# Linear attention with a routed feed-forward tree: keys turned by DMA, not by TensorE

## The chip, the cores and the metric

The kernel runs on one core of a Trainium2 chip. The metric is device time in microseconds of one execution. Matmuls run on TensorE (PE; PEld is its weight load), which writes PSUM; VectorE (DVE) and ScalarE (ACT) read PSUM and SBUF; GpSimd (POOL) works in SBUF alone; SyncE (SP) issues the DMAs.

## The reference, cut to what matters

`x` is 4 x 2048 x 256, fp32, with 16 heads of 64.

```python
xn = layernorm(x)
Q = phi(xn @ Wq + bq); K = phi(xn @ Wk + bk); V = xn @ Wv + bv      # phi = elu + 1
# causal linear attention, token by token, for each head:
KV += outer(k_i, v_i);  Ks += k_i
out_i = (q_i @ KV) / (q_i . Ks + 1e-6)
attn = out @ Wo + bo
# feed-forward: soft routing down a binary tree of depth 8
gate = sigmoid((xn @ Wq_tree.T) @ routers.T)
leaf_prob = products of gate or 1 - gate from the root to each of 256 leaves
ffn = (leaf_prob @ leaf_values) @ Wout.T + Wout_b
result = x + attn + ffn
```

## The kernel before, in words

**Tiling.** The 8192 tokens are 16 blocks (g) of 512. A block has 8 units (p), one for each pair of heads, so there are 128 units n = 8 g + p. Within a unit the 512 tokens are 8 chunks of 64. Projections are done as three products of split fp32 numbers (high x high, high x low, low x high) for each of two tiles of 128 inputs, six matmuls of 512 columns (`split_product`, L652 to L656).

**A unit on TensorE.** It begins with `tiled(n)` (L806), many 64 x 64 matmuls that use quarters of the array: the outputs from the running state (L765), the outer products of keys and values of unit n + 1 (L740, they read `k_tok`, keys with tokens on partitions), the scores of unit n + 1 (L729, they read `kT` and `qT`, features on partitions) and the outputs from the chunk itself (L779). Then comes the whole-array stretch: a hand-written list of fills, `unit_fills(g, p)` (L27), each the content of one of six PSUM banks: W0, W1 (w_pair), S0, S1 (s_pair), O0, O1 (o_pair). In order: a head fill on W1 (at p = 0 the product V1; at p = 1, 2 the transposes xT of the next block's input; at p = 3, 4 the transposes of the leaf probabilities; at p = 5, 6 a gate product), K of unit n + 2 on W0, Q of unit n + 2 on S0, a tail product of values on S1 (p = 0 to 6), kT of unit n + 2 on W0 (four transposes of the keys, L702) and oT on W1 (four transposes of this unit's output, L709). At p = 7 there is neither head nor tail; there oT comes ahead of the first of two long output products y (L667), and kT between the two.

**The other engines** work through the same list in their own queues, in order. ScalarE makes Relu (L407) and Exp (L410) for K and Q, the high half of what is to be split (L400, L430), the copy of the turned keys into `k_tok` (L420), and the copy of the scores into `aT` (L434). VectorE runs `carry(n + 1)` (L585, the running sums over eight chunks), `norm(n)` (L558 to L562), at p = 0 `normalise` (L506), then for each fill `phi` (L520), `low` (L512), `values` (L529) or `low_of_output` (L544). GpSimd masks the scores of unit n + 1 (L329, in two halves), adds the residual at p = 1 (L337), and at p = 7 works out the gates and all levels of the tree (L345 to L362). SP loads x and stores y.

**What sets the order.** Semaphores, counted by bank: `filled` when TensorE has finished a bank, `drained` when its last reader has. TensorE waits in `fill` (L673) for its bank to be drained, in `outer_products_when_ready` (L784) for kT and V, in `scores_when_ready` (L792) for Q and for both S banks, and in the second transpose of oT for the mask of the next unit (L705, L706):

```python
        for c in range(CH):
            if c == 1 and g * PAIRS + i + 1 < UNITS:
                until(a_masked, 2 * (g * PAIRS + i) + 4)
```

Of the kernel before, what the change touches and what calls it, by code (L numbers as in the profile page):

```python
# [7 lines left out]
F32 = mybir.dt.float32  # L8
F32R = mybir.dt.float32r

P = 128
# [15 lines left out]
def unit_fills(g, p, blocks):  # L27

    n = g * PAIRS + p
    ahead = divmod(n + 2, PAIRS) if n + 2 < blocks * PAIRS else None  # L30
# [12 lines left out]
    if p in (5, 6) and more:  # L43
        head, tail = [("gate", p - 5, g + 1)], [("V0", p - 3, g + 1)]

    fills = [(name, W1) for name in head]
    if ahead:
        fills += [(("K", ahead[1], ahead[0]), W0), (("Q", ahead[1], ahead[0]), S0)]
    fills += [(name, S1) for name in tail]
    if p == PAIRS - 1:  # L50

        fills += [(("oT", p, g), W1), (("y", 0, g), O1)]
    if ahead:
        fills.append((("kT", ahead[1], ahead[0]), W0))
    fills.append((("y", 1, g), S1) if p == PAIRS - 1 else (("oT", p, g), W1))
    return fills
# [4 lines left out]
         (("gate", 0, 0), S0), (("gate", 1, 0), S1), (("kT", 0, 0), W0), (("K", 1, 0), W0), (("Q", 1, 0), W1),  # L61
         (("kT", 1, 0), W0)]


def attention_and_tree_layer(nc, x, Wq, bq, Wk, bk, Wv, bv, Wo, bo,
# [45 lines left out]
    with ExitStack() as ctx:  # L111
# [36 lines left out]
        qT = sb("qT", [P, 2, TOK])  # L148
        ex = sb("ex", [P, 2, TOK])
        k_tok = sb("k_tok", [P, CH, P])  # L150
        aT = sb("aT", [P, 2, 2, CH, D])
        snaps = sb("snaps", [P, CHUNKS - 1, AUG])
# [30 lines left out]
        tree_cols = [xn[:, 0:2].rearrange("p c n -> p (c n)"), xn[:, 2:4].rearrange("p c n -> p (c n)"),  # L183
                     k_tok[:, :, :].rearrange("p c n -> p (c n)")]
        leafvT, woutT, routersT = [t.rearrange("p (t n) -> p t n", t=2) for t in tree_cols]
# [39 lines left out]
        a_masked = sem("a_masked")  # L225
        kv_filled = sem("kv_filled")
        sum_ready = sem("sum_ready")
        o_begun = sem("o_begun")
# [28 lines left out]
        def _(sp):  # L257
# [25 lines left out]

            for g in range(BLOCKS):
                if g + 2 < BLOCKS:
                    sp.wait_ge(x_consumed, g + 1)
                    sp.dma_start(x_in[:, g % 2], x_rows[g + 2]).then_inc(x_loaded[g % 2], 16)
                for i in range(2):
                    name = ("y", i, g)
                    sp.wait_ge(drained[bank_of[name]], count_of[name])  # L290
                    sp.dma_start(out_rows[g, :, 2 * i:2 * i + 2, :],
                                 y_buf[:, 2 * i:2 * i + 2, :]).then_inc(y_stored, 16)
            sp.wait_ge(y_stored, 32 * BLOCKS)

        @block.gpsimd
        def _(pool):
# [67 lines left out]
            FIRST_LEVELS = {0: range(0, 5), 1: range(5, 7), 2: range(7, depth)}  # L364

            mask(0)
            gates(0)
            pool.wait_ge(leaf_step, 1)  # L370
            for n in range(UNITS):
                g, p = divmod(n, PAIRS)
                if p == 0 and g + 1 < BLOCKS:
                    inverse_deviation(g + 1)
                    pool.wait_ge(rstd_ready, 2 * g + 4)
                if n + 1 < UNITS:
                    mask(n + 1)
                if p == 1:
                    residual(g)
                    pool.wait_ge(x_consumed, g + 1)  # L380
                if n in FIRST_LEVELS:
                    for l in FIRST_LEVELS[n]:
                        level(l, 0)
                    pool.wait_ge(leaf_step, 2 * FIRST_LEVELS[n][-1] + 3)
                if p == PAIRS - 1 and g + 1 < BLOCKS:
                    gates(g + 1)
                    for l in range(depth):
                        level(l, g + 1)
                    pool.wait_ge(leaf_step, (g + 2) * LEVEL_STEPS)

        @block.scalar
        def _(act):
# [25 lines left out]
            def copy_keys(name):  # L418
                act.wait_ge(filled[bank_of[name]], count_of[name])
                act.activation(k_tok[:, :, :].rearrange("p c n -> p (c n)"), psum_of(name), ACT.Copy)\  # L420
                   .then_inc(drained[bank_of[name]], 1)
# [45 lines left out]
            exponential(("Q", 1, 0))  # L467
            copy_keys(("kT", 1, 0))

            for n in range(UNITS):  # L470
                if n + 1 < UNITS:
                    copy_scores(n + 1)
                for name, _ in unit_fills(n // PAIRS, n % PAIRS, BLOCKS):
                    kind, i, g = name
                    if kind in "KQ":
                        exponential(name)
                    elif kind == "oT":
                        high_of_output(name)
                    elif kind == "kT":
                        copy_keys(name)  # L480
                    elif kind == "xT":
                        high(name, xnT[:, g % 2, 0, i])
                    elif kind == "leaf":
                        high(name, leafT[:, 0, i])
                    elif kind == "gate":
                        half_gates(name)

        @block.vector
        def _(dve):
# [25 lines left out]
            def phi(name):  # L515
                kind, p, _ = name
                slot, dst = (0, kT) if kind == "K" else (1, qT)
                col = p + (PAIRS if kind == "K" else 0)
                dve.wait_ge(exp_ready, exp_count[name])
                dve.scalar_tensor_tensor(out=dst[:, p % 2], in0=psum_of(name), scalar=bias_one[:, col:col + 1],  # L520
                                         in1=ex[:, slot], op0=ALU.add, op1=ALU.max)\
                   .then_inc(drained[bank_of[name]], 1)

            def values(name):
# [89 lines left out]
            carry(0)  # L614
            phi(("Q", 1, 0))

            for n in range(UNITS):
# [4 lines left out]
                if p == 0 and g + 1 < BLOCKS:  # L622
                    normalise(g + 1)
                fills = [name for name, _ in unit_fills(g, p, BLOCKS)]
                for name in values_first(fills, p):
                    kind, i, b = name
                    if kind in "KQ":
                        phi(name)
# [14 lines left out]
        def _(pe):  # L643
# [7 lines left out]

            def split_product(dst, lhs, rhs, tiles):  # L652
                steps = [s for t in range(tiles) for s in passes(lambda a, t=t: lhs(a, t), lambda a, t=t: rhs(a, t))]
                for i, (l, r) in enumerate(steps):
                    last = pe.matmul(dst, l, r, start=i == 0, stop=i == len(steps) - 1)  # L655
                return last  # L656
# [15 lines left out]

            def fill(name):  # L673
                kind, i, g = name
# [3 lines left out]
                if kind in "KQ":  # L678
                    wt = wk if kind == "K" else wq
                    last = split_product(dst, lambda a, t: wt[:, a, t, i * P:(i + 1) * P],  # L680
                                         lambda a, t: xnT[:, g % 2, a, t], KT_)
                elif kind in ("V0", "V1"):
                    half, n = int(kind[1]), 2 * HALF * D
                    last = split_product(dst, lambda a, t: xnT[:, g % 2, a, t, i * P:(i + 1) * P],
                                         lambda a, t: wv[:, a, t, half * n:(half + 1) * n], KT_)
                elif kind in ("xT", "leaf"):
# [13 lines left out]
                elif kind == "kT":  # L700
                    for c in range(CH):
                        last = pe.transpose(dst[:, c * P:(c + 1) * P], kT[:, i % 2, c * P:(c + 1) * P], ident[:, :])  # L702
                elif kind == "oT":
                    for c in range(CH):
                        if c == 1 and g * PAIRS + i + 1 < UNITS:  # L705
                            until(a_masked, 2 * (g * PAIRS + i) + 4)  # L706

# [76 lines left out]
            def outer_products_when_ready(n):  # L784
                g, p = divmod(n, PAIRS)
                until_drained(("kT", p, g))
                if p in (0, HALF):
# [87 lines left out]
            until_drained(("K", 1, 0))  # L875
            fill(("kT", 1, 0))
            until(split_lo_pool, len(LO_POOL))
            until(split_lo, len(LO_VECTOR))

            for n in range(UNITS):  # L880
                tiled(n)
                fills = unit_fills(n // PAIRS, n % PAIRS, BLOCKS)

                first_by_vector = fills[0][0][0] in ("V1", "xT", "leaf")
                for name, bank in fills:
# [12 lines left out]
                    if kind == "y" and i == 0:  # L898
                        for t in range(LT):
                            until_drained(("leaf", t, g))  # L900
                    if kind == "kT":
                        until_drained(("K", i, g))
                    fill(name)

# [24 lines left out]
```

## Time and profile before

| | |
|---|---|
| median of 3 runs | 1276.48 us (1273.93 to 1276.64) |
| the profiled execution, its own time | 1273.15 us |
| its span, first to last instruction | 1271.4 us |
| mean granted TensorE clock | 0.997 |
| busy: PE, PEld, DVE, ACT, POOL | 98%, 87%, 64%, 49%, 29% |

Busy shares are of the span. Matmuls are pipelined, so the duration drawn for one is longer than the distance to the next; the cost of a step on TensorE is read from the starts. "Idle before" in a row, in brackets, is how long the engine stood still ahead of the instruction, and for whom.

### The profile page before, as it was taken

What the parts mean: (1) busy time and instruction counts of PE and PEld (TensorE: products, weight loads), DVE (VectorE), ACT (ScalarE), POOL (GpSimd) and SP (SyncE); (2) the same over time, 40 slices, a digit from 0 to 9 for tenths busy, and PEclk for the clock granted to TensorE, in tenths of its full rate; (3) what the DMA queues carried; (4) which work ended last, traced back from release to release, by engine and by line L of the source; (5) the groups of instructions that cost most, each with busy time, mean ns of one, the idle gap of its engine ahead of it and who ended that gap; (6) DMA issues with size and microseconds to landing.
All of it is one profiled execution on the core that took longest, in us unless ns stands there. A gap on an engine that the chain in (4) does not pass through costs nothing.

```text
span 1271.4 us, 48688 instructions
## 1 busy us (share of the span) xinstructions
PE 1244.6 (98%) x22173; PEld 1105.0 (87%) x22173; DVE 810.3 (64%) x2186; ACT 622.4 (49%) x1007; POOL 374.3 (29%) x590
## 2 busy tenths in 40 slices
PE   5899999999999999999999999999999999999997
PEld 5789888898988989889898988989889898898986
DVE  4675766757576574765757666575765758657473
ACT  4563654536446363653636445364553636536361
POOL 3424232132421413223142321324214132231320
PEclk9899999999999999999999999999999999999999
DMA  6000001000000000001000010000000000000000
GB/s 223 19 3 19 19 2 35 3 18 20 10 28 3 19 19 10 28 3 36 2 19 19 3 35 3 19 20 10 28 3 19 19 18 20 2 19 3 19 3 18
DMA packets 21597, 25.91 MB, mean 20 GB/s; under 512 B 1025, under 2 KB 19728, under 8 KB 21392
## 3 DMA queue, kind: packets, MB, share of 16 engines
q1 hardware_dynamic: 21392, 22.82, 5.5%
q8 instruction: 173, 2.83, 0.9%
q14 instruction: 32, 0.26, 0.1%
HBM read 14.43 MB, written 8.39 MB: 18 GB/s over the span
## 4 chain that ended last, share of the span: by engine, by line
PE 97%; DVE 1%; ACT 1%; DMA 1%; SPq 0%; issue 0%; DVEq 0%
PE s_pair L655 25%; PE w_pair L655 20%; PE o_pair L667 9%; PE s_pair L667 9%; PE o_pair L765 6%; PE kv_pair L740 5%; PE o_pair L779 5%; PE s_pair L729 5%; PE w_pair L709 4%; PE w_pair L702 4%; PE w_pair L689 3%; DMA ffn_tok<-in_L_ffn_Wout_w_dram 1%; DVE snaps L585 0%; SPq L267 0%; PE o_pair L655 0%; ACT ex L407 0%
## 5 line engine op out<-in xcount | busy, mean ns | idle before, releaser
L329 POOL TENSOR_SCALAR_AFFINE_SELECT aT<-aT 64x512 f32<-64x512 f32 x256 | 167.6, 655 | 833.0 <-ACT aT L434 824.7
L655 PE MATMUL w_pair<-xnT,wk 128*128 128x512 f32 x768 | 205.7, 403 | 0.7 <-ACT k_tok L420 0.7
L655 PE MATMUL s_pair<-xnT,wq 128*128 128x512 f32 x756 | 194.0, 392 | 0.0
L434 ACT ACTIVATE aT<-s_pair 128x512 f32<-128x512 f32 x128 | 76.4, 597 | 238.3 <-PE s_pair L729 238.3
L585 DVE TENSOR_TENSOR snaps<-kv_pair,snaps 128x65 f32<-128x65 f32 x768 | 173.3, 226 | 26.4
L520 DVE SCALAR_TENSOR_TENSOR kT<-w_pair,bias_one,ex 128x512 f32<-128x512 f32 x128 | 96.2, 751 | 122.7 <-ACT ex L410 122.6
L655 PEld LDWEIGHTS s_pair<-xnT,wq 128*128 128x128 f32 x756 | 142.1, 188 | 31.4
L655 PE MATMUL s_pair<-wv,xnT 128*128 128x512 f32 x648 | 168.7, 395 | 0.0
L410 ACT ACTIVATE ex<-ex 128x512 f32<-128x512 f32 x256 | 161.8, 632 | 8.1
L407 ACT ACTIVATE ex<-w_pair,neg_bias 128x512 f32<-128x512 f32 x130 | 89.5, 689 | 148.5 <-PE w_pair L655 148.5
L655 PEld LDWEIGHTS w_pair<-xnT,wk 128*128 128x128 f32 x768 | 136.1, 188 | 26.6 <-ACT k_tok L420 1.0
L655 PEld LDWEIGHTS s_pair<-wv,xnT 128*128 128x128 f32 x648 | 121.6, 188 | 28.6
L420 ACT ACTIVATE k_tok<-w_pair 128x512 f32<-128x512 f32 x128 | 76.4, 597 | 143.0 <-PE w_pair L702 143.0
L520 DVE SCALAR_TENSOR_TENSOR qT<-s_pair,bias_one,ex 128x512 f32<-128x512 f32 x126 | 94.3, 748 | 59.6 <-ACT ex L410 59.6
L765 PE MATMUL o_pair<-snaps,qT 64*64 64x65 f32 x3584 | 112.2, 225 | 3.5 <-DVE state L585 3.5
L544 DVE TENSOR_TENSOR oT<-w_pair,oT 128x512 fp32r<-128x512 f32 x128 | 88.3, 690 | 27.4 <-ACT oT L430 27.4
L667 PE MATMUL o_pair<-wo,oT 128*128 128x256 f32 x768 | 94.7, 279 | 0.0
L667 PE MATMUL s_pair<-wo,oT 128*128 128x256 f32 x768 | 94.7, 279 | 0.0
L667 PEld LDWEIGHTS o_pair<-wo,oT 128*128 128x128 f32 x768 | 91.9, 188 | 0.0
L667 PEld LDWEIGHTS s_pair<-wo,oT 128*128 128x128 f32 x768 | 91.9, 188 | 0.0
L562 DVE TENSOR_TENSOR o_tok<-o_pair,rden 128x512 f32<-128x512 f32 x128 | 88.5, 691 | 4.4
L765 PEld LDWEIGHTS o_pair<-snaps,qT 64*64 64x64 f32 x3584 | 83.6, 135 | 8.7 <-issue 8.4
(105 smaller groups left out, 1953.7 us busy)
## 6 DMA issues: line engine op xcount, KB each, us to landing
x_in<-in_L_attn_x_dram SPq DMA_DIRECT2D x16, 512.0 KB, 3.9
out_dram<-y_buf SPq DMA_DIRECT2D x32, 256.0 KB, 2.1
stage<-in_L_attn_Wv_dram SPq DMA_DIRECT2D x2, 512.0 KB, 8.0
stage<-in_L_attn_Wk_dram SPq DMA_DIRECT2D x2, 512.0 KB, 9.6
stage<-in_L_attn_Wq_dram SPq DMA_DIRECT2D x2, 512.0 KB, 10.8
stage<-in_L_attn_Wo_dram SPq DMA_DIRECT2D x2, 512.0 KB, 9.1
bv_all<-in_L_attn_bv_dram SPq DMA_DIRECT2D x1, 512.0 KB, 8.6
ffn_tok<-in_L_ffn_Wq_dram SPq DMA_DIRECT2D x1, 256.0 KB
```

Source lines behind the costliest of these rows:

```text
L329: pool.affine_select(out=part, in_=part, compare_op=ALU.is_ge, fill=0.0, base=0, pattern=[[0, 2 * CH], [1, D]], channel_multiplier=-1).the ...
L407: act.activation(ex[:, slot], psum_of(name), ACT.Relu, scale=-1.0, bias=neg_bias[:, col:col + 1])\
L410: act.activation(ex[:, slot], ex[:, slot], ACT.Exp, scale=-1.0).then_inc(exp_ready, 1)
L420: act.activation(k_tok[:, :, :].rearrange("p c n -> p (c n)"), psum_of(name), ACT.Copy)\
L434: act.activation(aT[:, n % 2].rearrange("p h c q -> p h (c q)"), s_pair[:, :, 0:CH * D], ACT.Copy).then_inc(s_copied, 1)
L520: dve.scalar_tensor_tensor(out=dst[:, p % 2], in0=psum_of(name), scalar=bias_one[:, col:col + 1], in1=ex[:, slot], op0=ALU.add, op1=ALU.max)\
L544: dve.tensor_tensor(oT[:, 1, p], psum_of(name), oT[:, 0, p].bitcast(F32), ALU.subtract)\
L562: dve.tensor_tensor(o_tok[:, :, :, :].rearrange("p b t (h e) -> p b (t h) e", e=D), v[:, :, :, 0:D], rden[:, :, :].unsqueeze(3).to_broadca ...
L585: dve.tensor_tensor(dst, added, so_far, ALU.add).then_inc(sum_ready, 1)
L655: last = pe.matmul(dst, l, r, start=i == 0, stop=i == len(steps) - 1)
L667: last = pe.matmul(dst[:, (c % 2) * hid:(c % 2 + 1) * hid], oT[:, a, t, cols] if t < PAIRS else leafT[:, a, t - PAIRS, cols], wo[:, b, t] ...
L765: last = pe.matmul(output_at(t, h, a), qT[rows_of(h), p % 2, t * P + a * D:t * P + (a + 1) * D], before, start=turn == 0 and half not in b ...
```

## The change

The keys of units 2 and up no longer go through TensorE to be turned. K is projected one unit earlier (three units ahead of its use, not two) and is the first fill of each whole-array stretch, ahead of the head. When VectorE's `phi` has written `kT`, GpSimd takes the 32-bit numbers apart into two planes of 16-bit halves (`take_apart`), SP issues a DMA that transposes both planes (`turn_keys`), and VectorE interleaves the halves into `k_tok` (`put_together`), ahead of the first fill of an S bank in its list. TensorE waits for the mask ahead of the last matmul of the Q product, and for `put_together` ahead of the last matmul of the S1 product (at p = 7 after the first y). The first two units' keys are still turned by TensorE. SP's order is rewritten: stores of a block at the next block's first unit, the load of x at p = 2.

```diff
@@ unit_fills
-    fills = [(name, W1) for name in head]
-    if ahead:
-        fills += [(("K", ahead[1], ahead[0]), W0), (("Q", ahead[1], ahead[0]), S0)]
+    fills = [(("K", keys[1], keys[0]), W0)] if keys else []
+    fills += [(name, W1) for name in head]
+    if queries:
+        fills.append((("Q", queries[1], queries[0]), S0))
     fills += [(name, S1) for name in tail]
+    fills.append((("oT", p, g), W1))
     if p == PAIRS - 1:
-        fills += [(("oT", p, g), W1), (("y", 0, g), O1)]
-    if ahead:
-        fills.append((("kT", ahead[1], ahead[0]), W0))
-    fills.append((("y", 1, g), S1) if p == PAIRS - 1 else (("oT", p, g), W1))
+        fills += [(("y", 0, g), O1), (("y", 1, g), S1)]
@@ buffers
+        k_planes = sb("k_planes", [P, 2, TOK], U16)
+        k_turned = sb("k_turned", [P, 2 * CH, P], U16)
@@ SP
-            for g in range(BLOCKS):
-                if g + 2 < BLOCKS:
-                    sp.wait_ge(x_consumed, g + 1)
-                    sp.dma_start(x_in[:, g % 2], x_rows[g + 2]).then_inc(x_loaded[g % 2], 16)
+            def turn_keys(m):
+                sp.wait_ge(k_apart, m - 1)
+                if m > 2:
+                    sp.wait_ge(k_whole, m - 2)
+                sp.dma_start_transpose(k_turned[:, :, :], k_planes[:, :, :].rearrange("p s t -> p (s t)"))\
+                  .then_inc(k_turned_in, 16)
...
+            turn_keys(2)
+            for n in range(UNITS):
+                g, p = divmod(n, PAIRS)
+                if p == 0 and g:
+                    store(g - 1)
+                if n + 3 < UNITS:
+                    turn_keys(n + 3)
+                if p == 2 and g + 2 < BLOCKS:
+                    sp.wait_ge(x_consumed, g + 1)
+                    sp.dma_start(x_in[:, g % 2], x_rows[g + 2]).then_inc(x_loaded[g % 2], 16)
+            store(BLOCKS - 1)
@@ GpSimd
+            def take_apart(m):
+                g, p = divmod(m, PAIRS)
+                pool.wait_ge(drained[bank_of["K", p, g]], count_of["K", p, g])
+                if m > 2:
+                    pool.wait_ge(k_turned_in, 16 * (m - 2))
+                pool.tensor_copy(k_planes[:, :, :], kT[:, m % 2].bitcast(U16).rearrange("p (t s) -> p s t", s=2))\
+                    .then_inc(k_apart, 1)
+                pool.wait_ge(k_apart, m - 1)
...
                 if n + 1 < UNITS:
                     mask(n + 1)
+                if n + 3 < UNITS:
+                    take_apart(n + 3)
                 if p == 1:
                     residual(g)
@@ ScalarE
-                    elif kind == "kT":
-                        copy_keys(name)
@@ VectorE
+            def put_together(m):
+                dve.wait_ge(k_turned_in, 16 * (m - 1))
+                dve.wait_ge(kv_filled, m)
+                dve.tensor_copy(k_tok[:, :, :].rearrange("p c f -> p (c f)").bitcast(U16)
+                               .rearrange("p (n s) -> p s n", s=2),
+                               k_turned[:, :, :].rearrange("p (s c) f -> p s (c f)", s=2)).then_inc(k_whole, 1)
...
+                apart = True
                 for name in values_first(fills, p):
                     kind, i, b = name
+                    if apart and bank_of[name] in (S0, S1) and n + 2 < UNITS:
+                        put_together(n + 2)
+                        apart = False
@@ TensorE
-            def split_product(dst, lhs, rhs, tiles):
+            def split_product(dst, lhs, rhs, tiles, at_last=None):
                 for i, (l, r) in enumerate(steps):
+                    if at_last and i == len(steps) - 1:
+                        at_last()
...
-                        if c == 1 and g * PAIRS + i + 1 < UNITS:
-                            until(a_masked, 2 * (g * PAIRS + i) + 4)
...
-                until_drained(("kT", p, g))
+                if n < 2:
+                    until_drained(("kT", p, g))
+                else:
+                    until(k_whole, n - 1)
...
+                def masked():
+                    if n + 1 < UNITS:
+                        until(a_masked, 2 * n + 4)
+                def whole():
+                    if n + 2 < UNITS:
+                        until(k_whole, n + 1)
...
-                    if kind == "kT":
-                        until_drained(("K", i, g))
-                    fill(name)
+                    fill(name, masked if kind == "Q" else whole if bank == S1 and kind != "y" else None)
+                    if kind == "y" and i == 0:
+                        whole()
+                masked()
+                whole()
```

## Rows read from the trace of the kernel before

**Rows 1.** The page's part 1 (busy) and part 4 (the ending chain by line).
```profile
PE 1244.6 (98%) x22173; PEld 1105.0 (87%) x22173; DVE 810.3 (64%) x2186; ACT 622.4 (49%) x1007; POOL 374.3 (29%) x590
...
PE s_pair L655 25%; PE w_pair L655 20%; PE o_pair L667 9%; PE s_pair L667 9%; PE o_pair L765 6%; PE kv_pair L740 5%; PE o_pair L779 5%; PE s_pair L729 5%; PE w_pair L709 4%; PE w_pair L702 4%; PE w_pair L689 3%; DMA ffn_tok<-in_L_ffn_Wout_w_dram 1%; DVE snaps L585 0%; SPq L267 0%; PE o_pair L655 0%; ACT ex L407 0%
```

**Rows 2.** Timeline, one unit (p = 3): start us, us, engine, line, instruction.
```profile
608.33 0.27 PE L765 MATMUL o_pair<-state,qT 64*64 64x65 f32 x1
...
610.45 0.66 PE L689 MATMUL w_pair<-ident,ffn_tok 128*128 128x128 f32 x4
...
610.84 1.37 POOL L329 TENSOR_SCALAR_AFFINE_SELECT aT<-aT 64x512 f32<-64x512 f32 x2 [6.37 <-ACT aT L434]
610.86 1.63 PE L655 MATMUL w_pair<-xnT,wk 128*128 128x512 f32 x6
611.14 0.60 ACT L400 ACTIVATE leafT<-w_pair 128x512 fp32r<-128x512 f32 x1 [0.43 <-PE w_pair L689]
...
612.33 1.53 PE L655 MATMUL s_pair<-xnT,wq 128*128 128x512 f32 x6
612.47 0.68 DVE L512 TENSOR_TENSOR leafT<-w_pair,leafT 128x512 fp32r<-128x512 f32 x1
612.53 0.69 ACT L407 ACTIVATE ex<-w_pair,neg_bias 128x512 f32<-128x512 f32 x1 [0.79 <-PE w_pair L655]
613.25 0.63 ACT L410 ACTIVATE ex<-ex 128x512 f32<-128x512 f32 x1
...
613.70 1.56 PE L655 MATMUL s_pair<-wv,xnT 128*128 128x512 f32 x6
...
613.91 0.75 DVE L520 SCALAR_TENSOR_TENSOR kT<-w_pair,bias_one,ex 128x512 f32<-128x512 f32 x1 [0.77 <-ACT ex L410]
...
614.87 0.59 PEld L702 LDWEIGHTS w_pair<-ident,kT 128*128 128x128 f32 x4
615.10 0.60 PE L702 MATMUL w_pair<-ident,kT 128*128 128x128 f32 x4
615.29 0.75 DVE L520 SCALAR_TENSOR_TENSOR qT<-s_pair,bias_one,ex 128x512 f32<-128x512 f32 x1 [0.62 <-ACT ex L410]
...
615.53 0.60 PE L709 MATMUL w_pair<-ident,o_tok 128*128 128x128 f32 x4
...
615.95 0.68 DVE L529 TENSOR_TENSOR v_aug<-s_pair,bv_all 128x512 f32<-128x512 f32 x1
...
616.06 0.27 PE L765 MATMUL o_pair<-state,qT 64*64 64x65 f32 x1
```

**Rows 3.** Timeline of a p = 0 unit, TensorE and VectorE.
```profile
584.16 0.27 PE L765 MATMUL o_pair<-state,qT 64*64 64x65 f32 x1
...
592.86 0.27 PE L765 MATMUL o_pair<-state,qT 64*64 64x65 f32 x1
...
588.57 1.37 DVE L506 TENSOR_SCALAR xn<-x_in,mean_var,rstd 128x256 f32<-128x256 f32 x4
```

**Rows 4.** Groups by line and shape: count, busy us, mean ns.
```profile
L337 POOL TENSOR_TENSOR y_buf<-x_in,y_bias 128x1024 f32<-128x1024 f32 x16 | 38.7, 2419 | 1.3
...
L345 POOL TENSOR_SCALAR ffn_tok<-ffn_tok 128x1024 f32<-128x1024 f32 x16 | 17.6, 1102 | 1.4
...
L242 DVE TENSOR_TENSOR wk<-stage,wk 128x1024 fp32r<-128x1024 f32 x1 | 1.2, 1215 | 0.0
```

**Rows 5.** Timeline of the start, VectorE beside GpSimd.
```profile
37.63 1.38 POOL L329 TENSOR_SCALAR_AFFINE_SELECT aT<-aT 64x512 f32<-64x512 f32 x2 [7.20 <-ACT aT L434]
...
38.48 1.60 DVE L242 TENSOR_TENSOR wo<-stage,wo 128x1024 fp32r<-128x1024 f32 x1 [0.68 <-ACT wo L396]
...
39.10 1.89 POOL L345 TENSOR_SCALAR ffn_tok<-ffn_tok 128x1024 f32<-128x1024 f32 x1
```

**Rows 6.** The page's part 6: DMA issues, KB each, us to landing.
```profile
out_dram<-y_buf SPq DMA_DIRECT2D x32, 256.0 KB, 2.1
...
stage<-in_L_attn_Wq_dram SPq DMA_DIRECT2D x2, 512.0 KB, 10.8
```

More of the change, by code:

```diff
@@ L9 @@
 F32R = mybir.dt.float32r
+U16 = mybir.dt.uint16
 P = 128
@@ L29, in unit_fills @@
     n = g * PAIRS + p
-    ahead = divmod(n + 2, PAIRS) if n + 2 < blocks * PAIRS else None
+    keys = divmod(n + 3, PAIRS) if n + 3 < blocks * PAIRS else None
+    queries = divmod(n + 2, PAIRS) if n + 2 < blocks * PAIRS else None
     more = g + 1 < blocks
@@ L61 @@
          (("gate", 0, 0), S0), (("gate", 1, 0), S1), (("kT", 0, 0), W0), (("K", 1, 0), W0), (("Q", 1, 0), W1),
-         (("kT", 1, 0), W0)]
+         (("kT", 1, 0), W0), (("K", 2, 0), W0)]
 def attention_and_tree_layer(nc, x, Wq, bq, Wk, bk, Wv, bv, Wo, bo,
@@ L183, in attention_and_tree_layer @@
         tree_cols = [xn[:, 0:2].rearrange("p c n -> p (c n)"), xn[:, 2:4].rearrange("p c n -> p (c n)"),
-                     k_tok[:, :, :].rearrange("p c n -> p (c n)")]
+                     k_tok[:, :, :].rearrange("p c f -> p (c f)")]
         leafvT, woutT, routersT = [t.rearrange("p (t n) -> p t n", t=2) for t in tree_cols]
@@ L226, in attention_and_tree_layer @@
         kv_filled = sem("kv_filled")
+        k_apart = sem("k_apart")
+        k_turned_in = sem("k_turned_in")
+        k_whole = sem("k_whole")
         sum_ready = sem("sum_ready")
@@ L282, in _, with store @@
             load("wo1")
-            for g in range(BLOCKS):
-                if g + 2 < BLOCKS:
-                    sp.wait_ge(x_consumed, g + 1)
-                    sp.dma_start(x_in[:, g % 2], x_rows[g + 2]).then_inc(x_loaded[g % 2], 16)
+            def turn_keys(m):
[4 more added lines that the diff above has]
+                  .then_inc(k_turned_in, 16)
+            def store(g):
                 for i in range(2):
@@ L370, in _ @@
             pool.wait_ge(leaf_step, 1)
+            take_apart(2)
             for n in range(UNITS):
@@ L419, in copy_keys @@
                 act.wait_ge(filled[bank_of[name]], count_of[name])
-                act.activation(k_tok[:, :, :].rearrange("p c n -> p (c n)"), psum_of(name), ACT.Copy)\
+                act.activation(k_tok[:, :, :].rearrange("p c f -> p (c f)"), psum_of(name), ACT.Copy)\
                    .then_inc(drained[bank_of[name]], 1)
@@ L468, in _ @@
             copy_keys(("kT", 1, 0))
+            exponential(("K", 2, 0))
             for n in range(UNITS):
@@ L515, in phi @@
             def phi(name):
-                kind, p, _ = name
-                slot, dst = (0, kT) if kind == "K" else (1, qT)
+                kind, p, b = name
+                slot, dst = (0, kT[:, p % 2]) if kind == "K" else (1, qT[:, p % 2])
                 col = p + (PAIRS if kind == "K" else 0)
                 dve.wait_ge(exp_ready, exp_count[name])
-                dve.scalar_tensor_tensor(out=dst[:, p % 2], in0=psum_of(name), scalar=bias_one[:, col:col + 1],
+                dve.scalar_tensor_tensor(out=dst, in0=psum_of(name), scalar=bias_one[:, col:col + 1],
                                          in1=ex[:, slot], op0=ALU.add, op1=ALU.max)\
                    .then_inc(drained[bank_of[name]], 1)
+            def put_together(m):
[4 more added lines that the diff above has]
+                               k_turned[:, :, :].rearrange("p (s c) f -> p s (c f)", s=2)).then_inc(k_whole, 1)
             def values(name):
@@ L615, in _ @@
             phi(("Q", 1, 0))
+            phi(("K", 2, 0))
             for n in range(UNITS):
@@ L671, in output_rows, with fill @@
                 return last
-            def fill(name):
+            def fill(name, at_last=None):
                 kind, i, g = name
@@ L680, in fill @@
                     last = split_product(dst, lambda a, t: wt[:, a, t, i * P:(i + 1) * P],
-                                         lambda a, t: xnT[:, g % 2, a, t], KT_)
+                                         lambda a, t: xnT[:, g % 2, a, t], KT_, at_last)
                 elif kind in ("V0", "V1"):
@@ L684, in fill @@
                     last = split_product(dst, lambda a, t: xnT[:, g % 2, a, t, i * P:(i + 1) * P],
-                                         lambda a, t: wv[:, a, t, half * n:(half + 1) * n], KT_)
+                                         lambda a, t: wv[:, a, t, half * n:(half + 1) * n], KT_, at_last)
                 elif kind in ("xT", "leaf"):
@@ L701, in fill @@
                     for c in range(CH):
-                        last = pe.transpose(dst[:, c * P:(c + 1) * P], kT[:, i % 2, c * P:(c + 1) * P], ident[:, :])
+                        last = pe.transpose(dst[:, c * P:(c + 1) * P], kT[:, i, c * P:(c + 1) * P], ident[:, :])
                 elif kind == "oT":
                     for c in range(CH):
-                        if c == 1 and g * PAIRS + i + 1 < UNITS:
-                            until(a_masked, 2 * (g * PAIRS + i) + 4)
                         to = dst[:, c * P:(c + 1) * P].rearrange("p (a q) -> p a q", a=2)
@@ L876, in _ @@
             fill(("kT", 1, 0))
+            fill(("K", 2, 0))
             until(split_lo_pool, len(LO_POOL))
@@ L882, in _ @@
                 fills = unit_fills(n // PAIRS, n % PAIRS, BLOCKS)
-                first_by_vector = fills[0][0][0] in ("V1", "xT", "leaf")
+                first_by_vector = any(bank == W1 and name[0] in ("V1", "xT", "leaf") for name, bank in fills)
+                def masked():
[4 more added lines that the diff above has]
+                        until(k_whole, n + 1)
                 for name, bank in fills:
```

## The prediction

> **What bounds the kernel now.** I read the page first. TensorE is busy for 98% of the span, and the chain that ended last is made of TensorE's lines almost alone; the transposes of the keys (L702) hold 4% of it [rows 1]. VectorE is busy for 64%. So work taken from TensorE shortens the kernel one for one, until TensorE has to wait. Whether it will is a question of one unit's order in time, so I went to the timeline of a p = 3 unit [rows 2] and of a p = 0 unit [rows 3]. Count time there from the unit's first L765 matmul at 608.33, called 0. The leaf transposes start at 2.12, K at 2.53, Q at 4.00, V at 5.37, kT at 6.77, oT at 7.20, and the next unit at 7.73. Steps: transposes 0.41, K 1.47, Q 1.37, V 1.40, kT 0.43, oT 0.53. The reader is to see in the same rows the keys' path beside TensorE: K's first matmul to Relu 1.67, Relu to Exp 0.72, Exp to phi 0.66; phi starts 3.05 after K does. VectorE idles 0.77 ahead of it. There is slack in VectorE, but not at every place in its queue.
>
> **What the change removes.** 126 of the 128 kT fills on TensorE, 0.43 each by starts [rows 2]: 54 us in all. ScalarE's 126 copies to k_tok go too; ScalarE is half idle [rows 1], so I count nothing for them. Moving the wait for the mask from oT to Q's last matmul costs nothing: the mask starts at 2.51 and takes 1.37 [rows 2], so it ends at 3.88, while Q's last matmul now comes near 5.1.
>
> **What it adds.** Per unit: a GpSimd copy of 1024 16-bit elements, a transposing DMA of 256 KB, a VectorE copy of 1024 elements (`put_together`), and two waits. Three of these must be placed.
>
> *GpSimd.* 29% busy [rows 1]. The copy is bounded by 1.10 us (one input, 1024 elements) and 2.42 us (two inputs) [rows 4]; I take 1.10, the nearer form. Behind it in GpSimd's queue stand the next mask, wanted some 4 us later, and at p = 1 the residual add and at p = 7 the tree levels, which have units of time. It costs nothing by itself.
>
> *DMA and SP.* A 256 KB store lands after 2.1 us; the slowest large load, 512 KB in the crowded start, took 10.8 [rows 6]. No transposing DMA is in the trace. I take it near the store, since it is the same bytes at a quiet time. It is issued when the copy has ended and k_turned is free, near 7.7 of one unit, and wanted near 6.4 of the next, some 7.6 us later. Up to that it is hidden. SP's store waits for y, which is drained about a microsecond into p = 0, and the load at p = 2 stands behind a turn it doesn't need: both are in time. At p = 7 a unit lasts near 20 us and covers everything.
>
> *VectorE.* `put_together` stands in front of the first fill of an S bank, and TensorE now waits for it (k_whole) ahead of the last matmul of the S1 product. That is a wait within the same unit, for data that only the next unit's outer products need. Work out when it can end, at p = 3. K goes first, so it starts at 2.12 and phi(K) at 2.12 + 3.05 = 5.17. The low half of the leaf, which used to run at 4.14 ahead of phi, now stands behind it: two VectorE operations follow each other 0.66 apart for one of 0.75 (615.29 to 615.95) [rows 2], so it starts at 5.84, which ScalarE's copy (0.60, after Exp ends at 5.14) just allows. `put_together` starts 0.60 later, at 6.44. TensorE comes to V's last matmul at 2.12 + 1.47 + 0.41 + 1.37 + 5/6 of 1.40 = 6.54. So TensorE waits for nearly the whole copy, whatever that takes.
>
> Its price: no VectorE copy from SBUF to SBUF of this size is shown. The nearest row, 1024 elements in SBUF, is 1.22 us [rows 4]. Below it is the 0.68 of 512 elements [rows 2]. I take 1.22: the one single-input operation from SBUF to SBUF, L506, does four times 256 elements in 1.37 [rows 3], so one element a cycle of about 1 ns too. Then the copy ends at 7.66; from phi's end (614.66) to the weight load that waited for it are 0.21, and to the matmul 0.23 more [rows 2], so V's last matmul runs at 8.10, oT at 8.33, the next unit starts at 8.86. Against 7.73 that is 1.13 us longer.
>
> The Trainium skill (VectorE: DVE Perf Modes, the perf-mode tier table) says that an fp32 copy or tensor_scalar within SBUF handles two elements per cycle; the L506 row doesn't agree. An estimate by that table's rate is 0.69 us for this copy. The same skill (SBUF — State Buffer, Who interferes with whom) adds what speaks against the change: a VectorE operation in such a mode takes a port pair it shares with GpSimd as an exclusive lock. By both together the copy would wait for `take_apart` to end near 7.2 and itself end near 7.9, and the time would be about 1357.
>
> The trace shows such holding: a subtraction of 1.22 took 1.60 when it started inside a mask, and a GpSimd operation of 1.10 took 1.89 when it started inside that subtraction [rows 4, 5]. Here `take_apart` starts when phi(K) ends, near 6.05, and runs to 7.15, so a `put_together` that needs what GpSimd holds starts near 7.25 instead of 6.44: 0.81 more. A copy has one input, the held subtraction had two; I leave it out of the sum and keep it for the range.
>
> **By kind of unit**, in 16 blocks:
> - p = 1 to 4, 64 units with a low half on W1 or one like it: +1.13 each, +72.3.
> - p = 0, 16 units: `normalise` runs from 588.57 for 1.37 [rows 3], so phi(K) starts at 5.69, values at 6.35, the copy at 6.95; it ends at 8.17, the next unit starts at 8.17 + 0.21 + 0.23 + 0.23 + 0.53 = 9.37, against 8.70 (584.16 to 592.86): +0.67 each, +10.7.
> - p = 5, 6: the head is a gate product, drained by ScalarE; the copy runs from 5.84 to 7.06, and V's last matmul comes near 7.6. p = 7 has no S1 product to hold. 47 units at -0.43: -20.2.
>
> Sum +62.8. The profiled execution took 1273.15 (span 1271.40); 1273.15 + 62.8 = 1336. The median of the runs shown is 3.3 above that execution, so I say 1339.
>
> **Rivals.**
> *Short copy* (0.68, not held): copy ends at 7.12; p = 1 to 4 +0.59, p = 0 +0.13, the rest -0.43: +37.8 + 2.1 - 20.2 = +19.7, 1296. For it: 16-bit data; against it: L506.
> *Long copy, held and of full length*: +0.81 on 80 units, 65 more, 1404. If GpSimd's copy takes 2.42, a held short copy ends near 9.2, 1462.
> *The other side: the wait is already met.* If `put_together` can end before TensorE comes to V's last matmul, all 126 x 0.43 = 54 come out: 1222. It decides where the copy ends before 6.54 - 0.44 = 6.1 at p = 1 to 4. For it: VectorE has 0.77 idle ahead of phi(K) and 36% overall. Against it: its queue is in order, and even a copy of no length stands behind the low half, which ends at 6.4. Ordering or latencies would have to be half a microsecond better than in the rows.
> *Nothing in sum*: a very short copy, about 0.3: p = 1 to 4 +0.2, p = 0 -0.2, the rest -0.43; within 0.2%.
> *The DMA isn't hidden.* One transposition is under way at a time. If it takes 10.8, a unit needs 10.8 + some 0.8; 3.9 more at p = 1 to 4, 2.9 at p = 0, 5, 6: 24 a block, about 1650. It decides from 7.6 us on.
>
> **How the numbers follow.** The forecast's kind, 1310 to 1380: 0.50; short copy 0.18; held long or slow GpSimd, to 1460, 0.08; all saved 0.11; nothing in sum 0.05; DMA unhidden 0.08. The range is 1275 to 1460: it leaves out the two far cases, 0.19. A difference under 0.2% (2.6 us) can't be told from none by this measurement. Faster 0.11, same 0.05, slower 0.84.
>
> **What would show it.** In the profile after: TensorE below 98% with idle ahead of the S1 product's last matmul, put down to VectorE's `put_together`, in p = 0 to 4 and none in p = 5 to 7; units of 8.9 at p = 1 to 4 and 0.4 shorter ones at p = 5 and 6; L702 with 8 instructions; the new VectorE group with a mean of 1.2 (or 0.7, or more when held); a transposing DMA that lands under 7 us. Wrong if phi(K) doesn't start near 5.2, if the low half runs ahead of it, if the copy is far from 1.2, or if SP's waits name the DMA as the last to come.

## The result and the profile after

The changed kernel takes 1312.17 us (median of 4; 1309.35 to 1313.8), the kernel before 1276.56 beside it: ratio 1.0273, interval 1.0251 to 1.0295. It is slower by 36 us. I had said 1339, slower with a chance of 0.84, range 1275 to 1460. The profiled execution took 1312.1, with a span of 1310.3.

The page of the changed kernel: busy shares, the chain by engine, the two new copies and the new DMA (KB are not given for it; 3.1 is us to landing).

```profile
PE 1213.1 (93%) x21669; PEld 1040.4 (79%) x21669; DVE 923.1 (70%) x2312; ACT 552.0 (42%) x881; POOL 529.3 (40%) x716
...
PE 70%; DVE 19%; ACT 7%; issue 3%; DMA 1%; SPq 0%; POOL 0%; DVEq 0%; POOLq 0%
...
L396 POOL COPY k_planes<-kT 128x1024 uint16<-128x1024 uint16 x126 | 149.7, 1188 | 280.6 <-issue 228.9
...
L564 DVE COPY k_tok<-k_turned 128x1024 uint16<-128x1024 uint16 x126 | 133.8, 1062 | 0.0
...
k_turned<-k_planes SPq DMA_TRANSPOSE x126, 3.1
```

TensorE is busy 31.5 us less than in [rows 1], but its share fell from 98% to 93%, and the chain that ends last now runs through VectorE for 19%. Both new means are mixtures: VectorE's copy takes 1.24 in nearly all units of p = 0 to 4 and 0.75 in the others, GpSimd's 1.04 in the first and 1.43 in the second. The DMA lands well inside its time. The waits of the changed kernel, us in total, times, longest, put a name to the loss (PEld is the weight load of the same matmul, so the two lines are one wait):

```profile
PEld s_pair L707 <- DVE k_tok L564: 103.0, 78, 2.0
...
PE s_pair L707 <- DVE k_tok L564: 68.8, 77, 1.5
```

The idle drawn, 68.8 us, is less than what the waits cost, for the drawn length of a matmul runs past the start of the next: the kernel is near 39 us longer although 54 us were taken out, 93 in all.

Where in a unit it stands is seen in the timeline. This is a unit with the same fills as [rows 2] (p = 4 here, p = 3 there), from its first L816 matmul to the next unit's:

```profile
634.26 0.27 PE L816 MATMUL o_pair<-state,qT 64*64 64x65 f32 x1
...
636.28 1.65 PE L707 MATMUL w_pair<-xnT,wk 128*128 128x512 f32 x6
...
637.77 0.60 PE L742 MATMUL w_pair<-ident,ffn_tok 128*128 128x128 f32 x4
...
639.36 0.75 DVE L556 SCALAR_TENSOR_TENSOR kT<-w_pair,bias_one,ex 128x512 f32<-128x512 f32 x1 [0.94 <-ACT ex L447]
...
639.60 1.32 PE L707 MATMUL s_pair<-wv,xnT 128*128 128x512 f32 x5
...
640.02 0.68 DVE L548 TENSOR_TENSOR leafT<-w_pair,leafT 128x512 fp32r<-128x512 f32 x1
640.23 1.04 POOL L396 COPY k_planes<-kT 128x1024 uint16<-128x1024 uint16 x1 [2.17 <-issue]
...
640.62 1.24 DVE L564 COPY k_tok<-k_turned 128x1024 uint16<-128x1024 uint16 x1
...
641.92 0.51 PE L707 MATMUL s_pair<-wv,xnT 128*128 128x512 f32 x1 [0.99 <-DVE k_tok L564]
...
642.26 0.60 PE L760 MATMUL w_pair<-ident,o_tok 128*128 128x128 f32 x4
...
642.79 0.27 PE L816 MATMUL o_pair<-state,qT 64*64 64x65 f32 x1
```

Read it as the prediction counted, with 634.26 as 0. K starts at 2.02, phi of K at 5.10, the low half of the leaf at 5.76, VectorE's copy at 6.36; it ends at 7.60, and the last matmul of the S1 product, the lone L707 row with 0.99 of idle, starts at 7.66. The unit lasts 8.53 instead of 7.73. Two things were not in the sum: the matmul follows the copy's end by 0.06, and the copy's 1.24 is not its own length. GpSimd's copy runs from 640.23 to 641.27, and VectorE's, drawn from 640.62, ends 0.59 after that. In a p = 5 unit of the same execution VectorE starts first, and the roles change:

```profile
648.57 0.74 DVE L564 COPY k_tok<-k_turned 128x1024 uint16<-128x1024 uint16 x1
648.77 1.43 POOL L396 COPY k_planes<-kT 128x1024 uint16<-128x1024 uint16 x1 [2.18 <-issue]
```

There VectorE's copy takes 0.74, and it is GpSimd's that is drawn out, to 1.43. It ends 0.89 after VectorE's.

Unit lengths here and below run from a unit's first L816 matmul (L765 before) to the next unit's, and are medians over the blocks. For p = 0 to 7 they are 9.03, 8.54, 8.53, 8.72, 8.54, 8.22, 8.33 and 19.55; before they were 8.69, 7.73, 7.74, 7.73, 7.74, 8.77, 8.71 and 19.92. The sum per block is 2.43 us more, times 16 blocks 38.9 us, which is the difference between the two profiled spans (1310.3 and 1271.4).

### The profile page after: what moved, and what is told of

The parts are those of the page before. It is cut to its first block, busy times and chain, and to the rows that moved or that the text cites. A ratio compares the mean times of both kernels' runs of the same rounds, so it can differ in the third digit from the quotient of the medians.

```text
span 1310.3 us, 48282 instructions
## 1 busy us (share of the span) xinstructions
PE 1213.1 (93%) x21669; PEld 1040.4 (79%) x21669; DVE 923.1 (70%) x2312; ACT 552.0 (42%) x881; POOL 529.3 (40%) x716
## 4 chain that ended last, share of the span: by engine, by line
PE 70%; DVE 19%; ACT 7%; issue 3%; DMA 1%; SPq 0%; POOL 0%; DVEq 0%; POOLq 0%
PE w_pair L707 17%; PE s_pair L707 11%; PE o_pair L719 9%; PE s_pair L719 8%; DVE k_tok L564 7%; PE o_pair L816 6%; PE kv_pair L791 5%; PE w_pair L760 4%; PE o_pair L830 4%; PE s_pair L780 4%; ACT ex L444 4%; ACT ex L447 3%; DVE kT L556 3%; DVE snaps L629 2%; DVE leafT L548 2%
## 5 line engine op out<-in xcount | busy, mean ns | idle before, releaser
L396 POOL COPY k_planes<-kT 128x1024 uint16<-128x1024 uint16 x126 | 149.7, 1188 | 280.6 <-issue 228.9
L707 PE MATMUL s_pair<-wv,xnT 128*128 128x512 f32 x648 | 189.2, 407 | 68.8 <-DVE k_tok L564 68.8
L707 PEld LDWEIGHTS s_pair<-wv,xnT 128*128 128x128 f32 x648 | 121.5, 187 | 127.8 <-DVE k_tok L564 103.0
L707 PE MATMUL w_pair<-xnT,wk 128*128 128x512 f32 x768 | 211.9, 411 | 2.2 <-ACT k_tok L457 2.2
L707 PE MATMUL s_pair<-xnT,wq 128*128 128x512 f32 x756 | 200.9, 400 | 0.5 <-POOL aT L353 0.2
L707 PEld LDWEIGHTS w_pair<-xnT,wk 128*128 128x128 f32 x768 | 134.3, 188 | 34.2 <-ACT k_tok L457 2.7
L707 PEld LDWEIGHTS s_pair<-xnT,wq 128*128 128x128 f32 x756 | 135.2, 188 | 26.4 <-POOL aT L353 1.4
L467 ACT ACTIVATE oT<-w_pair 128x512 fp32r<-128x512 f32 x128 | 76.3, 596 | 148.7 <-PE w_pair L760 148.7
L564 DVE COPY k_tok<-k_turned 128x1024 uint16<-128x1024 uint16 x126 | 133.8, 1062 | 0.0
L816 PE MATMUL o_pair<-snaps,qT 64*64 64x65 f32 x3584 | 113.4, 224 | 0.3 <-DVE state L629 0.3
L444 ACT ACTIVATE ex<-s_pair,neg_bias 128x512 f32<-128x512 f32 x126 | 86.8, 689 | 49.4 <-PE s_pair L707 49.0
L573 DVE TENSOR_TENSOR v_aug<-s_pair,bv_all 128x512 f32<-128x512 f32 x108 | 74.5, 690 | 30.1 <-PE s_pair L707 30.1
```

Source lines behind the costliest of these rows:

```text
L396: pool.tensor_copy(k_planes[:, :, :], kT[:, m % 2].bitcast(U16).rearrange("p (t s) -> p s t", s=2))\
L444: act.activation(ex[:, slot], psum_of(name), ACT.Relu, scale=-1.0, bias=neg_bias[:, col:col + 1])\
L564: dve.tensor_copy(k_tok[:, :, :].rearrange("p c f -> p (c f)").bitcast(U16) .rearrange("p (n s) -> p s n", s=2), k_turned[:, :, :].rearran ...
L816: last = pe.matmul(output_at(t, h, a), qT[rows_of(h), p % 2, t * P + a * D:t * P + (a + 1) * D], before, start=turn == 0 and half not in b ...
```

## The experiments

The theory after the result: TensorE is held ahead of the S1 product's last matmul by VectorE's interleaving copy, which is late because of its place in VectorE's queue, and later still because whichever of the two 16-bit copies starts second is held by the first. The rivals: the added work on VectorE and GpSimd is the bound wherever it stands; the transposing DMA is late or disturbs; the order of the fills or the move of the mask's wait does it. The kernel before, timed beside them, took 1277.03 for the first four experiments and 1276.33 for the other four.

### The wait, put where the keys are used

```diff
-                    fill(name, masked if kind == "Q" else whole if bank == S1 and kind != "y" else None)
-                    if kind == "y" and i == 0:
-                        whole()
+                    fill(name, masked if kind == "Q" else None)
                 masked()
-                whole()
```

> The changed kernel, with TensorE's wait for the interleaved keys only where they are used (outer products of the next unit), not ahead of the S1 product's last matmul. My theory (TensorE is held in the same unit by a copy that ends 7.6 us into a p = 1 to 4 unit): the 1.0 us of idle ahead of that matmul goes; the outer products come at 7.6 and hardly wait, but Q and V are then drained only at 8.2 and 8.9, and the scores, wanted at 8.4, wait about 0.6 in its place. So a unit of 7.9 to 8.0 instead of 8.5: about 35 us less, 1270 to 1285. Rival (VectorE's and GpSimd's load is the bound, wherever the wait stands): 1305 to 1315.

1265.9 us, ratio 0.9906 (0.9883 to 0.9929): 46 us less than the changed kernel, 4 below the range that I gave, and about 1% faster than the kernel before. So the wait's place cost that much. What is left is seen in its timeline, where a p = 3 unit starts at 604.02 while VectorE is still at the unit before:

```profile
604.02 0.27 PE L816 MATMUL o_pair<-state,qT 64*64 64x65 f32 x1
...
604.26 0.67 DVE L573 TENSOR_TENSOR v_aug<-s_pair,bv_all 128x512 f32<-128x512 f32 x1
...
604.86 0.74 DVE L556 SCALAR_TENSOR_TENSOR qT<-s_pair,bias_one,ex 128x512 f32<-128x512 f32 x1
...
605.08 0.70 PE L791 MATMUL kv_pair<-v_aug,k_tok 64*64 64x65 f32 x32 [0.60 <-DVE v_aug L573]
...
612.12 0.27 PE L816 MATMUL o_pair<-state,qT 64*64 64x65 f32 x1
```

The outer products (L791) have 0.60 of idle; they wait there for the values that VectorE writes last (604.26, 0.67). The unit lasts 8.10; those of p = 1, 2 and 4 last 7.50, 7.95 and 7.96. The scores, which I expected to wait 0.6, wait 0.2 at most. VectorE's copy is still late (it still takes 1.25) and pushes phi of Q and the values behind it into the next unit. The wait in the unit was a cost of its own, but a late copy costs without it too.

### The copy, put first in VectorE's list

```diff
                 fills = [name for name, _ in unit_fills(g, p, BLOCKS)]
-                apart = True
+                if n + 2 < UNITS:
+                    put_together(n + 2)
                 for name in values_first(fills, p):
                     kind, i, b = name
-                    if apart and bank_of[name] in (S0, S1) and n + 2 < UNITS:
-                        put_together(n + 2)
-                        apart = False
```

> The changed kernel, with put_together ahead of all of VectorE's fills of the unit (right behind norm or normalise), nothing else. My theory (the place of the copy in VectorE's queue is the cause): the copy runs near 4.2 us into the unit, in VectorE's idle time, outside GpSimd's copy, takes 0.75, and TensorE's wait is met long before. Nearly all of 54 us comes out against the kernel before: 1222 to 1235. Rival 1 (VectorE's load or the shared hold is the bound): above 1280. Rival 2 (the transposing DMA is too late for this place, since it lands some 3 us into the unit at best): units bound by the DMA chain, 8 us or more, above 1270.

1229.04 us (1228.92 to 1235.26), ratio 0.9633 (0.9605 to 0.9662): 83 us less than the changed kernel and 48 less than the kernel before. Nothing else was moved: VectorE, GpSimd and the DMAs have the same instructions, and the order of the fills on TensorE is the changed one. That rules out their load, the DMA and that order as what cost the time. The timeline from the copy of a p = 3 unit to the starts of the p = 4 and the p = 5 unit:

```profile
593.50 0.75 DVE L564 COPY k_tok<-k_turned 128x1024 uint16<-128x1024 uint16 x1
...
594.52 0.75 DVE L556 SCALAR_TENSOR_TENSOR kT<-w_pair,bias_one,ex 128x512 f32<-128x512 f32 x1 [0.28 <-ACT ex L447]
...
595.19 0.68 DVE L548 TENSOR_TENSOR leafT<-w_pair,leafT 128x512 fp32r<-128x512 f32 x1
595.40 1.04 POOL L396 COPY k_planes<-kT 128x1024 uint16<-128x1024 uint16 x1 [2.19 <-issue]
...
596.16 0.60 PE L757 MATMUL w_pair<-ident,o_tok 128*128 128x128 f32 x4
...
596.69 0.27 PE L813 MATMUL o_pair<-state,qT 64*64 64x65 f32 x1
...
604.07 0.27 PE L813 MATMUL o_pair<-state,qT 64*64 64x65 f32 x1
```

The copy (593.50, 0.75) now lies in the idle time ahead of phi of K, and GpSimd's (595.40, 1.04) far behind it. oT follows the S1 product with no wait, and the unit from 596.69 to 604.07 lasts 7.38. The prediction's nominal 7.30 differs by 0.08; per block 2.97 us come out, of the 3.4 that the removed transposes would give by 0.43 each.

### GpSimd's copy listed with the next unit

```diff
+                if n and n + 2 < UNITS:
+                    take_apart(n + 2)
                 if n + 1 < UNITS:
                     mask(n + 1)
-                if n + 3 < UNITS:
-                    take_apart(n + 3)
```

> The changed kernel, with GpSimd's take_apart of unit n + 2 at the start of unit n's GpSimd work, ahead of the mask, so that it is far from VectorE's copy. My theory (in p = 0 to 4 VectorE's copy of 0.74 us takes 1.24 because it starts inside GpSimd's copy and is held until that ends): the copies are 0.74 everywhere, 80 units are 0.5 shorter, 1265 to 1280. Rival (1.24 is the copy's own length in these units, or DMA traffic makes it so): copies stay at 1.24, 1305 to 1315. If the DMA, issued 3 us into the unit at worst, lands too late, VectorE waits for it and the time rises.

1306.99 us, ratio 1.0232 (1.0204 to 1.0259): 5 less than the changed kernel, whose interval it overlaps (1.0251 to 1.0295), and in the range of the rival. As a test of the hold it failed, by my mistake: GpSimd has nothing in front of it and reaches the copy as soon as the keys are drained, still in the unit before. An entry moved in a queue that idles is not moved in time. Only at p = 1, behind the residual add, and at p = 7, behind the tree levels, is GpSimd kept back. The timeline shows a p = 1 unit's copies and then, for comparison, those of p = 2:

```profile
611.97 0.73 DVE L564 COPY k_tok<-k_turned 128x1024 uint16<-128x1024 uint16 x1
611.98 1.62 POOL L396 COPY k_planes<-kT 128x1024 uint16<-128x1024 uint16 x1
...
612.76 0.50 PE L707 MATMUL s_pair<-wv,xnT 128*128 128x512 f32 x1 [0.49 <-DVE k_tok L564]
...
619.62 1.04 POOL L396 COPY k_planes<-kT 128x1024 uint16<-128x1024 uint16 x1 [2.18 <-issue]
...
620.01 1.24 DVE L564 COPY k_tok<-k_turned 128x1024 uint16<-128x1024 uint16 x1
...
621.31 0.50 PE L707 MATMUL s_pair<-wv,xnT 128*128 128x512 f32 x1 [1.00 <-DVE k_tok L564]
```

At p = 1 VectorE starts 0.01 ahead of GpSimd and takes 0.73, GpSimd 1.62; the matmul waited 0.49 and the unit lasts 8.01 instead of 8.52. At p = 2, with GpSimd ahead, the copy takes 1.24 and the matmul waits 1.00, as before. In 14 of the 16 units of p = 1 the two copies start within 0.03 of each other, and only one of them is drawn out: in eight it is GpSimd's (1.62 to 1.65) and VectorE's takes 0.73 or 0.74; in six it is VectorE's (1.60), GpSimd's takes 1.04 and the unit lasts 8.9. The first kind ends 0.89 after the other copy, the second 0.59. This speaks for the hold.

### Every turn issued twice

```diff
+                sp.dma_start_transpose(k_turned[:, :, :], k_planes[:, :, :].rearrange("p s t -> p (s t)"))\
+                  .then_inc(k_spare_in, 16)
+                sp.wait_ge(k_spare_in, 16 * (m - 1))
                 sp.dma_start_transpose(k_turned[:, :, :], k_planes[:, :, :].rearrange("p s t -> p (s t)"))\
                   .then_inc(k_turned_in, 16)
```

> The changed kernel, with each transposing DMA issued twice in turn, the second after the first has landed, so the keys come some 3 us later and the DMA work is doubled. My theory (the DMA is hidden; it has 7 us and takes 3.1): no change, 1308 to 1316. Rival (the transposing DMA or its traffic costs the time): each of seven units in eight 1 to 3 us longer, above 1400.

1340.6 us, ratio 1.0488 (1.0456 to 1.052): 28 more than the changed kernel. Both expectations missed; mine was that it is free. Its waits name GpSimd's copy behind the DMA (us, times, longest), and the timeline shows one such place:

```profile
POOL k_planes L400 <- DMA k_turned<-k_planes: 144.0, 45, 5.1
```

```profile
621.11 1.24 SPq L297 DMA_TRANSPOSE k_turned<-k_planes  x1
...
625.70 1.91 SPq L300 DMA_TRANSPOSE k_turned<-k_planes  x1
...
629.17 0.74 DVE L568 COPY k_tok<-k_turned 128x1024 uint16<-128x1024 uint16 x1 [0.77 <-DMA k_turned<-k_planes]
629.29 1.51 POOL L400 COPY k_planes<-kT 128x1024 uint16<-128x1024 uint16 x1 [3.54 <-DMA k_turned<-k_planes]
```

The first turn is issued at 621.11, the second at 625.70, 4.6 later instead of 3.1, and the keys are there near 629.1, 8.0 after the first issue. VectorE waited 0.77 and GpSimd 3.54, and since both are let go by the same landing, they meet again and GpSimd's copy is held (1.51). So the time from issue to use is near 7 to 8 us: one turn of 3.1, or 4.9 at most, fits in it with room, two don't always. That was the flaw in my expectation: twice 3.1 already fills most of it. Why a turn sometimes takes 4.6 I haven't found. For the changed kernel itself the DMA is hidden; its VectorE never waits for it.

### GpSimd's copy only after VectorE's

```diff
                 if m > 2:
                     pool.wait_ge(k_turned_in, 16 * (m - 2))
+                    pool.wait_ge(k_whole, m - 2)
```

> The changed kernel, with one more wait in take_apart: GpSimd copies unit n + 3's keys only after put_together of unit n + 2, so the two copies never overlap. The theory of the hold: VectorE's copy takes 0.74 in every unit, ends 0.5 earlier in 80 units, and the time falls by about 40 to 1272 (1265 to 1280). Rival (the copy is 1.24 long in p = 0 to 4 for another reason): 1305 to 1315. The DMA is issued some 0.6 us later and stays hidden.

1275.45 us (10 runs), ratio 0.9995 (0.9982 to 1.0007): 37 less than the changed kernel, by one added wait, and level with the kernel before. The timeline of a p = 2 unit:

```profile
605.57 0.73 DVE L565 COPY k_tok<-k_turned 128x1024 uint16<-128x1024 uint16 x1
...
606.36 0.50 PE L708 MATMUL s_pair<-wv,xnT 128*128 128x512 f32 x1 [0.49 <-DVE k_tok L565]
606.47 1.04 POOL L397 COPY k_planes<-kT 128x1024 uint16<-128x1024 uint16 x1 [3.08 <-DVE k_tok L565]
```

VectorE's copy takes 0.73, GpSimd's starts behind it and takes 1.04, and the matmul's idle is 0.49 where it was 1.00. Over all 126 the means are 0.75 and 1.04. The hold is shown: it was 0.5 us in each of 80 units, 40 us, close to all that the changed kernel lost. The 0.49 that is left, for a copy that is still late in VectorE's queue, is why this kernel is level with the one before and not at 1229.

### The mask's wait moved, in the kernel before

```diff
-                        if c == 1 and g * PAIRS + i + 1 < UNITS:
-                            until(a_masked, 2 * (g * PAIRS + i) + 4)
...
-                    fill(name)
+                    fill(name, masked if kind == "Q" else None)
+                masked()
```

> The kernel before, with only its wait for the mask moved from oT's second transpose to the last matmul of the Q product. The mask ends 3.9 us into the unit, ahead of both places. Mine: no difference, within 3 us of the kernel before. Rival (a wait among short instructions costs issue time, about 0.1 us a unit): 8 to 15 us faster.

1275.74 us (12 runs), ratio 0.9995 (0.9982 to 1.0008): no difference within 0.2%. That part of the change is neutral.

### The head ahead of the keys again

```diff
-    fills = [(("K", keys[1], keys[0]), W0)] if keys else []
-    fills += [(name, W1) for name in head]
+    fills = [(name, W1) for name in head]
+    if keys:
+        fills.append((("K", keys[1], keys[0]), W0))
```

> The changed kernel, with the head fill ahead of the keys again, as in the kernel before, all else as changed. K comes 0.41 later at p = 1 to 4, but the low half of the head then runs ahead of phi, so VectorE's copy starts near 6.25, not later than now, and ahead of GpSimd's copy, which starts 0.13 after phi ends. By the theory (order in VectorE's queue, and the hold by whichever starts first) the copy takes 0.74 and ends near 7.0 instead of 7.6: 1262 to 1280. Rival (projecting the keys first is what makes them early enough, and doing it later costs): 1312 to 1340.

1281.39 us (10 runs), ratio 1.0037 (1.0023 to 1.0052): 31 less than the changed kernel, just outside my range. The timeline of a p = 2 unit:

```profile
607.86 0.68 DVE L549 TENSOR_TENSOR xnT<-w_pair,xnT 128x512 fp32r<-128x512 f32 x1
...
609.28 0.75 DVE L557 SCALAR_TENSOR_TENSOR kT<-w_pair,bias_one,ex 128x512 f32<-128x512 f32 x1 [0.74 <-ACT ex L448]
609.94 0.74 DVE L565 COPY k_tok<-k_turned 128x1024 uint16<-128x1024 uint16 x1
...
610.15 1.43 POOL L397 COPY k_planes<-kT 128x1024 uint16<-128x1024 uint16 x1 [2.49 <-issue]
...
610.74 0.50 PE L708 MATMUL s_pair<-wv,xnT 128*128 128x512 f32 x1 [0.35 <-DVE k_tok L565]
```

With the low half already done (607.86), VectorE's copy follows phi of K directly and starts 0.21 ahead of GpSimd's; it takes 0.74, GpSimd's 1.43, and the matmul waits 0.35. Units of p = 1 to 4 last 7.8 to 8.0. At p = 5 and 6, where the head is a long product, K is now later and they last 8.8 each (8.22 and 8.33 in the changed kernel), which is where the rest of the gain went. Projecting the keys first was no gain with this queue of VectorE's: it put the low half between phi and the copy.

### Copy first and wait at the use

The edits of the first two experiments together.

> put_together ahead of all fills, as in e2, and TensorE's wait only where the keys are used, as in e1. By the theory the wait in the unit is already met in e2 in all units, so its removal changes nothing: 1226 to 1233. Rival (some of p = 0's or p = 2's units still stand at it): 2 to 8 us less than e2.

1231.55 us, ratio 0.9655 (0.9637 to 0.9673): not distinguishable from the copy first alone (1229.04; its interval ends at 0.9662). With the copy early, the wait in the unit costs nothing, so it may stay.

## Why the prediction was right, and what was off

**The step that decided held.** The prediction put a wait ahead of the S1 product's last matmul in p = 0 to 4 and none in p = 5 to 7, for a copy that starts 6.44 us into a p = 3 unit and ends at 7.66. Measured (p = 4): 6.36 and 7.60. The waits name it, and taking it away (first experiment) or moving its cause (second) gives 46 and 83 us back. The DMA never makes VectorE wait in the changed kernel, and the mask's wait costs nothing, as said; the last was tried alone. That GpSimd's copy "costs nothing by itself" was wrong: its queue has the time, but where it meets VectorE's copy it cost 37 us.

**The size was too large, +62.8 in the sum against +38.9 between the two profiled spans, and 1339 against 1312.** Term by term, by unit: p = 1 to 4 was +1.13 each, measured +0.81, +0.79, +0.99 and +0.80; p = 0 was +0.67, measured +0.34; p = 5 to 7 was -0.43 each, measured -0.55, -0.38 and -0.37. The mis-sized term in all of p = 0 to 4 is the release: I took 0.21 from VectorE's end to a weight load and 0.23 more to the matmul. Both are from a place in [rows 2] where TensorE had a product in progress and the row shows no wait, so they were no time of release; here TensorE stands idle, and 0.06 pass. That is 0.38 too much in each of 80 units, 30 us. From that matmul to oT 0.34 pass and not 0.23, which takes 0.11 back, and the copy ends 0.06 earlier than in the sum. A p = 0 unit shows the same (copy at 6.87 for 6.95, next unit at 9.04 for 9.37):

```profile
520.25 0.27 PE L816 MATMUL o_pair<-state,qT 64*64 64x65 f32 x1
...
527.12 1.24 DVE L564 COPY k_tok<-k_turned 128x1024 uint16<-128x1024 uint16 x1
...
529.29 0.27 PE L816 MATMUL o_pair<-state,qT 64*64 64x65 f32 x1
```

At p = 3 a further 0.19 is lost, which was not in the sum. VectorE takes the values ahead of phi of Q at p = 2, and both are late; the next unit's outer products start right behind the values, and K comes 2.21 into that unit instead of 2.02:

```profile
625.21 0.69 DVE L573 TENSOR_TENSOR v_aug<-s_pair,bv_all 128x512 f32<-128x512 f32 x1 [0.59 <-PE s_pair L707]
...
625.54 0.27 PE L816 MATMUL o_pair<-state,qT 64*64 64x65 f32 x1
...
625.96 0.69 PE L791 MATMUL kv_pair<-v_aug,k_tok 64*64 64x65 f32 x32
```

**The copy's 1.22 was right by luck.** I took a rate of one element a cycle from L506, which is four instructions of 256 elements in a row and says little of one of 1024. The copy alone is 0.74, near the estimate of 0.69 that I worked out from the Trainium skill's table (VectorE: DVE Perf Modes, the perf-mode tier table), and it is drawn as 1.24 because GpSimd's copy is in front of it. The prediction had both pieces in sight, the rate and the exclusive lock on the shared ports (Trainium skill, SBUF — State Buffer, Who interferes with whom), with an end near 7.9, and left both out of its sum. By that rule the one that starts second waits for the first: the traces agree both ways, VectorE's end is 0.59 after GpSimd's at p = 4, GpSimd's 0.89 after VectorE's at p = 5, and there is no trace of it when they don't meet (0.75 and 1.04). Both tails are 0.15 shorter than the copy alone, and GpSimd's copy ended at 7.01 and not at 7.15, so the end came at 7.60. With 0.74 and no hold the same sum gives about 1301.

**The other side was closer than I gave it.** "All saved" was put at 1222 and needed the copy to end before 6.1. The change as made didn't do so, but the same instructions in another order took 1229. I had seen the 0.77 of idle ahead of phi as slack that the queue couldn't use; it is exactly the place for the copy, whose data has landed by then.

**One rival was summed wrongly.** "Nothing in sum" with a copy of 0.3 comes, by its own terms, to 64 x 0.2 - 16 x 0.2 - 20.2 = -10.6, which is 0.8% faster and not within 0.2%.

## What to carry to other kernels

When work moves from the bounding engine to another, place it in that engine's queue by when its input is there and its output is wanted, not by where the list has a convenient gap: here one line's place was worth 83 us. A wait on the bounding engine for data that is used only later turns the helper's lateness into a stall at once. Before two copies within SBUF go to VectorE and GpSimd, look whether they meet in time; one wait that keeps them apart gave 37 us.

## What the runs showed of the hardware

- A VectorE copy of 128 x 1024 16-bit elements within SBUF, written at every second element, takes 0.74 us; a GpSimd copy of the same size, read at every second element, takes 1.04. Where they meet, the one that starts second is drawn out: VectorE's to 1.24 when it starts 0.4 behind and 1.60 when they start together, GpSimd's to 1.43 when it starts 0.2 behind and 1.62 to 1.65 together. VectorE's then ends 0.59 after GpSimd's, GpSimd's 0.89 after VectorE's.
- A transposing DMA of 128 x 1024 16-bit elements within SBUF lands 3.1 us after its issue (median of 126, at most 4.9), and holds SP for 1.23.
- A matmul held by a semaphore while TensorE is idle starts 0.06 after the signal's instruction ends (78 of 78 such waits in the changed kernel), with its weight load drawn at the same time.
